# A ViT block's first batch: two tiles of queries turned by TensorE, keys of two tiles turned behind the first exps

## The reference, cut to what matters

```python
h = einsum('bhid,oi,od->bho', x, weighted_sum, weight)
q, k, v = split(layernorm(h) @ qkv_w.T + qkv_b)      # 16 heads of 16
q, k = rotate(q), rotate(k)
q = q / max(norm(q), EPS); k = k / max(norm(k), EPS)
attn = softmax(einsum('bhqd,bhkd->bhqk', q, k) * SCALE)
h = h + einsum('bhqk,bhkd->bhqd', attn, v) @ out_w.T + out_b
f = sum over e of weights[:, e] * (relu(ln(h) @ W1[e] + b1[e]) @ W2[e] + b2[e])
out = h + f                                          # weights: gated sigmoid
```

## Time and profile before

| | us |
|---|---|
| median of 3 runs | 1910.03 (1909.69 to 1910.92) |
| profiled execution, its own time | 1907.93 |
| its span | 1906.1 |
| PE busy | 1834.9 |
| ACT busy | 1077.5 |
| DVE busy | 697.6 |
| POOL busy | 629.4 |

### The profile page before, as it was taken

One profiled execution on the slowest core, in us unless ns is written; L12 is line 12 of the kernel. 1 busy time (PEld: TensorE's weight loads), 2 busy tenths in 40 slices (PEclk: granted clock), 3 DMA queues, 4 the chain that ended last, 5 costly groups with the idle time before them and its releaser, 6 DMA issues.

```text
span 1906.1 us, 31838 instructions
## 1 busy us (share of the span) xinstructions
PE 1834.9 (96%) x12652; PEld 1166.2 (61%) x12652; DVE 697.6 (37%) x1575; ACT 1077.5 (57%) x1658; POOL 629.4 (33%) x537
## 2 busy tenths in 40 slices
PE   5688999999999999999999999999999999999999
PEld 4156545775467754777457764577546775466666
DVE  7858645452123610336004450145402352121001
ACT  3744776546654576545664466544665546654444
POOL 1012323334233332333323342333423334234443
PEclk9789999999999999999999999999999999999999
DMA  4332542515123331334213251231512315113221
GB/s 164 113 109 89 147 164 89 188 67 133 67 89 100 100 100 67 111 100 106 95 67 111 100 133 47 107 113 56 133 67 89 122 68 133 67 67 110 101 102 43
DMA packets 103971, 192.31 MB, mean 101 GB/s; under 512 B 67448, under 2 KB 80656, under 8 KB 87440
## 3 DMA queue, kind: packets, MB, share of 16 engines
q1 hardware_dynamic: 103824, 190.28, 30.8%
HBM read 153.55 MB, written 20.97 MB: 92 GB/s over the span
## 4 chain that ended last, share of the span: by engine, by line
PE 83%; DVE 3%; ACT 3%; DMA 2%; issue 2%; SPq 0%; DVEq 0%; ACTq 0%
PE bank_h L994 31%; PE bank_f L1013 11%; PE bank_f L1015 10%; PE bank_f L1016 10%; PE bank_o L902 6%; PE bank_s L888 4%; PE bank_s L800 3%; PE bank_s L801 3%; PE bank_s L802 3%; DMA kt<-probs 1%; ACT hh L777 1%; DMA kt<-stack 1%; DVE acc L1254 1%; DMA raw<-in_w_dram 1%; PE bank_s L948 1%
## 5 line engine op out<-in xcount | busy, mean ns | idle before, releaser
L643 POOL TENSOR_TENSOR hl<-h,hh 128x512 f16<-128x512 f32 x512 | 602.7, 1177 | 1192.9 <-ACT hh L777 685.3
L994 PE MATMUL bank_h<-x,w1s 128*128 128x512 f16 x3072 | 749.0, 380 | 5.0 <-ACT hh L777 4.4
L774 ACT ACTIVATE h<-bank_h,b1s 128x512 f32<-128x512 f32 x512 | 351.3, 686 | 468.5 <-PE bank_h L994 468.3
L1013 PE MATMUL bank_f<-w2s,hh 128*128 128x256 f16 x2048 | 560.4, 274 | 0.8 <-DVE acc L1254 0.8
L1015 PE MATMUL bank_f<-w2s,hh 128*128 128x256 f16 x2048 | 558.7, 273 | 0.0
L1016 PE MATMUL bank_f<-w2s,hl 128*128 128x256 f16 x2048 | 558.7, 273 | 0.0
L994 PEld LDWEIGHTS bank_h<-x,w1s 128*128 128x128 f16 x3072 | 287.3, 98 | 330.2 <-issue 39.5
L777 ACT ACTIVATE hh<-bank_h,b1s 128x512 f16<-128x512 f32 x512 | 350.0, 684 | 0.0
L743 ACT ACTIVATE probs<-bank_s 128x1024 f32<-128x1024 f32 x240 | 246.4, 1026 | 167.3 <-PE bank_s L888 166.3
L1013 PEld LDWEIGHTS bank_f<-w2s,hh 128*128 128x128 f16 x2048 | 201.5, 98 | 105.0 <-issue 38.8
L1254 DVE SCALAR_TENSOR_TENSOR acc<-bank_f,gw,acc 128x256 f32<-128x256 f32 x256 | 106.2, 477 | 369.5 <-PE bank_f L1016 369.4
(11 more groups left out here) (187 smaller groups left out, 1436.5 us busy)
## 6 DMA issues: line engine op xcount, KB each, us to landing
w1s<-w_parts SPq DMA_DIRECT2D x56, 1024.0 KB, 4.8
w2s<-w_parts SPq DMA_DIRECT2D x56, 1024.0 KB, 4.8
raw<-in_w_dram SPq DMA_DIRECT2D x16, 1024.0 KB, 6.6
xraw<-in_x_t_dram SPq DMA_DIRECT2D x30, 512.0 KB, 4.8
w_parts<-w1s SPq DMA_DIRECT2D x8, 1024.0 KB, 8.6
w_parts<-w2s SPq DMA_DIRECT2D x8, 1024.0 KB, 10.5
out_dram<-acc SPq DMA_DIRECT2D x16, 256.0 KB, 6.1
w1s<-in_x_t_dram SPq DMA_DIRECT2D x2, 512.0 KB, 8.2
```

What stands on the lines that cost most here:

```text
L643: pool.tensor_tensor(hl[n % HBUFS][:], h32[n % 2][:], hh[n % HBUFS][:], ALU.subtract)\
L774: act.activation(h32[n % 2][:], bank_h[n % 2][:, :], ACT.Relu, bias=b1s[:, e, m:m + 1]).then_inc(h_hi.sem, 1)
L994: last = pe.matmul(bank_h[n % 2][:, :], w[:, wp, k, m * P:(m + 1) * P], x16s[fb % 2][:, xp, k, :], start=(k == 0 and wp + xp == 0), stop=( ...
L1013: pe.matmul(o, high, w[:, 0, m, :], start=(m == 0 and t % 2 == 0), stop=False, skip_group_check=True)
```

## The change

Three things are changed in batch 0 alone. Queries of tiles 2 and 3 are turned by TensorE (`query_turn`, into `bank_m` and `bank_o`) and copied by ACT (tile 2) and DVE (tile 3), and SP turns only tiles 0 and 1. The turns and copies of key tiles 2 and 3 move behind `scores 1` and `scores 3`, and the step `projections 1` moves behind `scores 1` with them; the scores of a key tile now wait for that tile alone. The signal `stack_turned[0]` still counts 16 for each query tile.

```diff
-                 "key_turn 0", "key_copy 0", "unit 3", "stack 2", "key_turn 1", "key_copy 1", "stack 3", "key_turn 2",
-                 "key_copy 2", "key_turn 3", "key_copy 3", "projections 1"]
+                 "key_turn 0", "key_copy 0", "unit 3", "stack 2", "query_turn 2", "stack 3", "query_copy 2",
+                 "query_turn 3", "query_copy 3", "key_turn 1", "key_copy 1"]
...
-    between = {("scores", 0): [("maxima", 0), ("maxima", 1), ("reduce", 0), ("scales", 0),
+    between = {("scores", 1): [("key_turn", 2), ("key_copy", 2), ("projections", 1)],
+               ("scores", 3): [("key_turn", 3), ("key_copy", 3)],
+               ("scores", 0): [("maxima", 0), ("maxima", 1), ("reduce", 0), ("scales", 0),
                                ("parts", 0), ("parts", 1), ("parts", 2), ("parts", 3)],
...
+        queries_turned = sem("queries_turned")
...
+        def query_bank(t):
+
+            return (bank_m, bank_o)[t % 2][:, :].bitcast(F16).rearrange("p (h t) -> p h t", t=P)
...
-            turn_stacks(0, range(TT))
+            turn_stacks(0, range(TT // 2))
...
+                elif stage == "query_copy" and n == 2:
+                    wait(act, stack_turned[0], ab, 16)
+                    act.wait_ge(queries_turned, 1)
+                    copy(qt[:, :, n * P:(n + 1) * P], query_bank(n)).then_inc(stack_turned[0].sem, 16)
...
+                elif stage == "query_turn":
+                    wait(pe, stack_ready, ab, 2 * n + 1)
+                    for h in range(HEADS // 2):
+                        last = pe.transpose(query_bank(n)[:, h, :],
+                                            stack_of(ab, n)[:, 0, 2 * h:2 * h + 2].rearrange("p h s d -> p (h s d)"),
+                                            hl[0][:, 0:P])
+                    last.then_inc(queries_turned, 1)
                 elif stage == "scores":
                     (g, tile), half = divmod(n // 2, TT), n % 2
+                    if fb is None and g == 0 and half == 0:
+                        wait(pe, stack_turned[1], ab, 16 * (tile + 1))
                     if n == 0:
-                        for turned in stack_turned:
-                            wait(pe, turned, ab, 16 * TT)
+                        wait(pe, stack_turned[0], ab, 16 * TT)
+                        if fb is not None:
+                            wait(pe, stack_turned[1], ab, 16 * TT)
...
+                elif stage == "query_copy" and n == 3:
+                    wait(dve, stack_turned[0], ab, 16)
+                    dve.wait_ge(queries_turned, 2)
+                    dve.tensor_copy(qt[:, :, n * P:(n + 1) * P], query_bank(n)).then_inc(stack_turned[0].sem, 16)
```

## The result

| | before | changed |
|---|---|---|
| median, us (10 runs each) | 1909.94 | 1915.64 |
| profiled execution's span | 1906.1 | 1912.8 |

The ratio is 1.0029, 95% interval 1.002 to 1.0038: slower by 5.7 us, against a forecast of 5.85, and inside the forecast's range (1912.5 to 1918.0). In the experiments, the median of queries_only leaves out one slow execution of 1956.59 us, with a mean granted clock of 0.94 in place of 0.99.

What follows compares the result with a forecast made beforehand. TensorE bounds the span, but in the first batch step order sets the time. First weighing +4.75 and clock +1.1 give +5.85 us on 1910.03: 1915.9, range 1912.5 to 1918.0.

Steps and rivals of the forecast that it cites:

- The head: Start of attention: without the wait for DMA query transposes, scores start at 59.8, exp 0 at 60.5, 4.8 us earlier.
- DVE's query copy: Copy of query tile 3 from PSUM ahead of the scores: 1.2 us taken, bounds 0.75 and 1.7.
- The standstill on the path: GpSimd's 6.97 us gap behind the all-reduce now precedes the adds on V; `weigh 0` at 72.55, 4.75 us later.
- my two pieces of evidence: In GpSimd's gap, a config pair (67.1) and an instruction-queue packet (about 70 us), read as a change of code.
- The adds: GpSimd's four adds on V behind `reduce 0`: 0.73 us each; `weigh 0` waits for the first.
- DVE's fourth scaling: On DVE, may stand behind the five GpSimd adds in a row: 2.85 us in place of 0.75.
- The clock: TensorE's pause before `weigh 0` delays its rise to 2.4 GHz, 6.4 us counted from there: 1.1 us extra, up to 2.0.
- Given back?: After exp 4 and in the next batch: nothing with its own due time was found to absorb the +5.85 us.
- My reading of DVE's slack: Later groups: with TensorE some 6 us later and DVE less, TensorE's turns find DVE's divisions done.
- the standstill wasn't `out_bias`'s own: Rival: GpSimd's gap belongs to `out_bias`, not the switch; `weigh 0` 2.15 us earlier, -3.2, 1906.8; chance 0.06.
- the adds do gate: Rival: adds on V gate nothing, whole gain shows; `weigh 0` 3.5 us earlier, -3.9, 1906.1; chance 0.02.
- nothing of the loss came back: Rival, partly given back: a shorter load or unseen slack takes 2 to 4 us; +3, 1913.0; chance 0.10.

Runs made afterwards that it cites:

- queries_only: Changed kernel with keys 2 and 3, their copies and `projections 1` back ahead of the scores; 1912.57 us against 1910.24, ratio 1.0011.
- dve_quiet: Changed kernel with DVE held from the parts of expert 0's weights until GpSimd's adds on V are done; 1915.69 us, one execution.
- adds_last: Kernel before, with only GpSimd's four adds on V moved behind the all-reduce; 1917.42 us, ratio 1.0038.

## Why the prediction was right

**The head.** Right: exp 0 is 5.0 us sooner from the mark (forecast 4.8). DVE's query copy took 0.69, not 1.2: with its source in PSUM it was no slower than the scaling from SBUF (0.75), so my lower bound was the right one. The scores start 5.3 us sooner, but exp 0 stands behind ACT's copy of key 1 (from 58.87, 1.02 us), which takes 0.3 of that back.

**The standstill on the path.** Right in place and size. All-reduce at 63.3 (forecast 64.4, of which 0.5 each is the copy and the run's earlier start), 7.01 us, then the adds. It carried over from `out_bias` to another instruction, stood between the last of two all-reduces and the add, and stayed with DVE idle; putting the adds ahead took it off the path, putting them behind in the old kernel brought it on. One of my two pieces of evidence was worthless, though: the instruction-queue packet at 70 us. In the changed kernel none moves between 63 and 71 us, while the config pair stands at 63.7:

```profile
L655 POOLq MODIFY_POOL_CONFIG  x2: 83/83/83, 63.7 to 63.7; - x2
```

That code is loaded in it is thus argued, from the config pairs, and not shown. The Trainium skill, GPSIMD Engine Reference, section Instruction dispatch, gives 5.95 us for a first call after a load. The standstills of all thirteen profiled executions lie between 6.74 and 7.31 us, so the kind of cost agrees and the figure is 0.8 to 1.4 us low for this kernel.

**The adds.** Mis-sized: 0.73 us by the row, 1.05 to 1.71 with DVE at work, and about 1.1 for the first, the only one that is in the sum. The 0.35 more and the 0.5 less of the copy nearly cancel, which was luck: the weighing came 4.60 late from the mark, against 4.75. DVE's fourth scaling, which I thought might be held up to 2.85 us, took 1.22.

**The clock.** Right in size: exp 6 is 5.85 late, exp 4 4.61, so the extra is 1.24 (forecast 1.1). But the step to it, that the clock rises some 6.4 us after the weighings begin, was partly luck. It rose after 5.2 us here, after 2.7 in dve_quiet and 2.9 in adds_last (3.2 before), and in adds_last the extra was nil. I also hadn't seen that the clock would rise at 60.1 and fall again. When it comes back after a pause isn't settled by these runs.

**Given back?** No: 5.74 at the attention's end, 5.7 in the medians. My reading of DVE's slack held for a TensorE that comes later. For one that comes sooner it was half a microsecond, and each variant that gained at the head lost part of it there. The rivals fell: the standstill wasn't `out_bias`'s own, the adds do gate, and nothing of the loss came back.

## What to carry to other kernels

When steps are moved in a list that all engines walk, follow each engine's share apart: here 7 to 9 us turned on four small adds in a step named after something else. On GpSimd, keep what others wait for ahead of a change of instruction kind, and look for a standstill that costs nothing today before moving work behind it. After speeding up one engine's stretch, look for the engine that was just in time: moving its work elsewhere in the queue helps only if it goes to where it idles.

## What the hardware showed beyond expectation

- DVE copied 128x1024 fp16 from PSUM in 0.69 us, where 128x256 fp32 took 0.42: more columns per microsecond, at half the bytes each.
- GpSimd's 128x256 add took 0.72 us with DVE idle, 1.05 to 1.71 beside DVE's scalings. DVE was held up in turn: a scaling took 1.22 us beside the adds on V, in place of 0.75, and a 24x256 operation 2.39 beside `out_bias`, in place of 0.40.
- A pause of 9 us of TensorE cost 2.2 us in this stage by the clock alone, and filling it with matmuls nobody needs gave them back.
- Two all-reduces in a row had one standstill behind them, not two.
